# Expert rows that carry their destination: the per-tile results of a mixture of experts scattered by GpSimd instead of gathered per batch

## The chip, the cores and the metric

The kernel runs on one core of a Trainium2 chip. The metric is the device time of one launch in microseconds, the median of several runs. The engines of a core work side by side and meet at semaphores: TensorE (PE, with its weight loads PEld), VectorE (DVE), ScalarE (ACT), GpSimd (POOL) and SyncE (SP, which only starts transfers). 16 DMA engines move the data.

## The reference

The input is 16 batches of 256 tokens of 128 numbers. Four layers follow, each with a residual and a layer norm:

```
x = norm(x + attention0(x))     # MLP in front, 16 heads of 64, keys up to 63 ahead of the query
x = norm(x + experts(x))        # 16 experts, the best 4 of each token, 128 -> 512 -> 128, gelu
x = norm(x + attention1(x))     # 16 heads of 8, projections with a low-rank part, full softmax
x = norm(x + recurrent(x))      # gated state carried over the batches, tanh output
```

The expert layer computes, for each token, four expert results and their sum weighted by a softmax of the four router values.

## The kernel before

**Stage A, first attention and routing (about 30 to 671 us of the profile).** A loop over 16 batches `b`, each in eight steps `p` (a pair of heads each). In a step PE computes the scores of the pair (L804), the next q and k (L752, L753), in even steps the output projection of two older pairs (L821, which reads `OT`), the transposes of the normalized `P` of the step before (L841), and in odd steps P times V (L859). DVE copies `PTA` to `PT` (L1323), in even steps then `OTB` to `OT` (L1327), takes minima and shifted scores (L1335), and gives `rinv` (L1349, L1369). ACT takes the exponentials (L1165). POOL multiplies `P` by `rinv` (L555, three instructions in a step; PE's L841 of the next step waits for them). In steps 3 to 7 the finished batch is normalized and routed: DVE finds the four experts of a token (`hot`), its rank in each and from that its row in `xs` (`pos`), a table in DRAM with a region for each expert, and in step 7 writes `pos`, `pos_all` and the gates `gate_all` (L1411, L1413). In steps 0 to 3 of the following batch POOL issues eight indirect DMAs that scatter the 128-number rows of `x1c` to `xs` (L545, two in a step, ahead of the step's `P`).

**Stage B, experts (about 693 to 975 us).** DVE plans 144 tiles of 128 rows of one expert. SP loads a tile of rows (`load_rows`, L423), PE transposes it (L905) and multiplies it with the expert's two matrices (L917 and, two tiles later, L928). DVE copies the weights (`wA`, `wB`; L1487, L1490), the transposed rows (L1494), and adds the bias to the result `yrow` (L1516). SP stores `yrow` back over the same rows of `xs` (`store_rows`, L429). POOL clears buffers for stage C, one piece a tile, and gathers the results of batches 0 to 3 with indirect DMAs, paced by DVE's tile counter (L599). SP stores and loads the first stack of stage C at tiles 95 and 98 to 102.

**Stage C, second attention and recurrent layer (about 975 to 1417 us).** A loop over batches with eight steps of two heads. q and k of batch `b + 2` are split into three bf16 parts, stored to DRAM (`store_parts`, L439, four DMAs), and read back as a stack (`load_stack`, L446 to L456, nine DMAs into `qst`, `kst` or, for every third batch, into a part of `wall`). The scores of the next iteration start when the stack has landed (L1029); its step 1 computes the next q and k (L981), so stack, projection, parts, store and load are a loop. POOL's `outputs` fetches eight blocks of 128 expert results for one batch (`fetch`, L599, four at a time), ACT weighs them (L1241), POOL sums them (`combine`).

SP, POOL and the other engines take their instructions in order, so an instruction that waits holds all behind it. Two waits matter here:

```
DVE tile(n): need(dve, "hid_ready", 4 * n - 4); weights_A; rows_T; yrow of tile n - 2; weights_B
DVE tile(n): need(dve, "ys_out", tile n - 6)    # four yrow buffers
```

Of the kernel before, what the change touches and what calls it, by code (L numbers as in the profile page):

```python
# [36 lines left out]
LEVELS = TOK // GT  # L37
WA = F + FC
# [74 lines left out]
def build(nc, t, out):  # L113
    ctx = ExitStack()
    with ctx:
# [13 lines left out]
        pos_all = sb("pos_all", [128, B * TT * TOPK], u32)  # L129
# [10 lines left out]
        upto = sb("upto", [128, LEVELS])  # L140
        ended = sb("ended", [128, 2, LEVELS])
        spent = sb("spent", [128, 2, LEVELS])
# [9 lines left out]
        plan = sb("plan", [1, 512], i32)  # L152
        zrow = sb("zrow", [128, D])
        minus_half = sb("minus_half", [128, 8])

# [8 lines left out]
        hT = sb("hT", [128, TOK], c=a)  # L164
        h1 = sb("h1", [128, 2, 512], c=a)
# [13 lines left out]
        x1c = sb("x1c", [128, TT, D], c=a)  # L179
# [34 lines left out]
        lesser = sb("lesser", [128, LEVELS, E], c=a)  # L214
        a.close()
# [27 lines left out]
        posc = sb("posc", [128, 2, TT * TOPK // 2], u32)  # L243
# [16 lines left out]
        xg = sb("xg", [128, 4, D], c=e2)  # L260
# [3 lines left out]
        hid = sb("hid", [128, 4, FC, GT], c=e2)  # L264
        yrow = sb("yrow", [128, 4, D], c=e2)
# [25 lines left out]
        def rows_of(b):  # L291

            return h1[:, 0, :].rearrange("q (i d) -> q i d", d=D)[:, 0:TT, :] if isinstance(b, int) and b == B - 1 else x1c

        xs = nc.dram_tensor("xs", (ROWS, D), fp32, kind="Internal").ap()
# [7 lines left out]
            var_ready pow_ready x1c_ready m_x x1T_ready m_l mask_ready m_r pos_ready xsq_ready x1_kept scat exp_w top_ready  # L303
            ksq_ready rmat_ready b2_kept a_done plan_ready zrow_ready plan_out plan_in filled
# [3 lines left out]
            yk_in0 yk_in1 gates_in weighed comb_done var2_ready pow2_ready posc_ready xo_kept h_full fin_dve fin_pool var3_ready pow3_ready scale_ready h_act fin_ready out_done""".split()  # L308
# [65 lines left out]
        def _(sp):  # L374
# [17 lines left out]
            nothing = zrow[:, :].rearrange("q (o d) -> q o d", o=1).to_broadcast([128, E, D])  # L392
            for c in range(CAP // 128):
                if c % 2 == 0 and c > 0:
                    sp.wait_ge(s["filled"], 16 * c)
                if c >= 4:
                    sp.wait_ge(s["wo_mm"], PAIRS * (c // 2 - 1))
                sp.dma_start(rows[128 * c:128 * c + 128, :, :], nothing).then_inc(s["filled"], 16)
            sp.dma_start(xs[DUMMY:ROWS, :].rearrange("(e r) d -> r e d", r=128), nothing[:, 0:NT - FULL, :]).then_inc(s["filled"], 16)
# [9 lines left out]
            sp.dma_start(plan[:, :], plan_d.rearrange("(o t) c -> o (t c)", o=1)).then_inc(s["plan_in"], 16)  # L409
            sp.wait_ge(s["plan_in"], 16)  # L410
            sp.wait_ge(s["filled"], 16 * (CAP // 128 + 1))
# [6 lines left out]
            row = {}  # L418

            def load_rows(n):  # L420
                need_alone(sp, "tin_mm", n - 3)
                row[n] = row_of(n)
                sp.dma_start(xg[:, n % 4, :], xs[bass.ds(row[n], GT), :]).then_inc(s[f"xg_in{n % 4}"], 16)  # L423

            def store_rows(n):

                need_alone(sp, "yrow_ready", n + 1)
                need_alone(sp, f"ys_out{n % 2}", 16 * (n // 2))
                sp.dma_start(xs[bass.ds(row[n], GT), :], yrow[:, n % 4, :]).then_inc(s[f"ys_out{n % 2}"], 16)  # L429
# [11 lines left out]
            def load_stack(b, load, pair):  # L441

                if pair == 0:
# [3 lines left out]
                for w, x in ((1, kst), (0, qst)):  # L447
                    dst = x[load][2 * DH1 * pair:2 * DH1 * (pair + 1), :, :].rearrange("q (e h) n -> q e (h n)", e=2)
                    rows = qkd[w].rearrange("e a (d h) n -> (a d) e (h n)", h=H1 // 2)
                    first, second = PRODUCTS[pair][0][w], PRODUCTS[pair][1][w]  # L450
                    if first == second:
                        for e in range(2):
                            src = rows[DH1 * first:DH1 * (first + 1), e, :].rearrange("(o q) n -> o q n", o=1).to_broadcast([2, DH1, H1 // 2 * N])
                            sp.dma_start(dst[:, e, :], src).then_inc(s["stk"], 16)  # L454
                    else:
                        sp.dma_start(dst, rows[DH1 * first:DH1 * (second + 1), :, :]).then_inc(s["stk"], 16)  # L456

            for n in range(4):
                row[n] = row_of(n)
            sp.wait_ge(s["scat"], 16 * B * TT * TOPK)  # L460
            for n in range(4):
                sp.dma_start(xg[:, n, :], xs[bass.ds(row[n], GT), :]).then_inc(s[f"xg_in{n}"], 16)
            for n in range(NT + 4):
# [9 lines left out]
                if n in (98, 100, 102):  # L473
                    load_stack(-2, 0, (n - 98) // 2)

            def attention(b, par):
                if has(b, 2):
# [3 lines left out]
                    for qa in range(NPART):  # L481
                        load_stack(b, (par + 2) % 3, qa)
# [1242 lines left out]
```

## Time and profile before

| what | value |
|---|---|
| median of 3 runs | 1420.69 us (1418.19 to 1424.83) |
| the profiled execution | 1418.6 us, span 1416.9 us |
| busy in the span | PE 1261.3, PEld 969.5, DVE 1021.7, ACT 931.6, POOL 774.8 us |
| DMA | 110.98 MB, q1 (SP) 22.4% and q0 (POOL) 4.2% of 16 engines' span |
| chain that ended last | PE 25%, DMA 11%, SP's queue 6%, DVE 5% of the span |

The time that a row gives is from the span's start. A row of the timeline has start, length, engine, line, operation, tiles and count, and in brackets the idle time before it and what ended that. The chain of work that ended last is followed back from the last instruction; what stands in it at a time is what held the end there.

### The profile page before, as it was taken

To read this page: it belongs to the slowest core of one execution; us is meant where nothing else is said; L and a number is where in the kernel's file an instruction comes from. 1 tells how busy PE (TensorE), PEld (TensorE's weight loads), DVE (VectorE), ACT (ScalarE), POOL (GpSimd) and SP (SyncE) were. 2 spreads that over 40 slices of the span, in tenths; PEclk is the share of its full clock that TensorE was granted. 3 is DMA by queue.
4 is the path that set the end of the run, shared out by engine and by line. 5 is a ranking of instruction groups with operands and counts; after the bars stand their busy time and mean duration, and the time that the engine had idled before them with its cause. 6 is when DMAs were issued, how large, how long until landed. Compare 5 with 4: busy or idle time off the path is not lost.

```text
span 1416.9 us, 36694 instructions
## 1 busy us (share of the span) xinstructions
PE 1261.3 (89%) x9756; PEld 969.5 (68%) x9756; DVE 1021.7 (72%) x3767; ACT 931.6 (66%) x2827; POOL 774.8 (55%) x983
## 2 busy tenths in 40 slices
PE   7999999999999999996699999898687888888884
PEld 3777777677767777764599999897355555556552
DVE  1677777777777777775677777577678887878845
ACT  5877777777778777774366666464456665666554
POOL 1557777777777777775331131215547777674232
PEclk9999999999999999998799999999789999999997
DMA  9612222111222222221122222323223232322102
GB/s 338 219 61 76 74 74 74 59 43 54 70 73 71 74 74 74 74 71 50 45 72 74 82 81 79 93 75 82 67 70 82 64 85 52 91 58 74 40 2 60
DMA packets 149016, 110.98 MB, mean 78 GB/s; under 512 B 12833, under 2 KB 137249, under 8 KB 148770
## 3 DMA queue, kind: packets, MB, share of 16 engines
q1 hardware_dynamic: 139842, 92.45, 22.4%
q0 software_dynamic: 8192, 16.79, 4.2%
q8 instruction: 46, 0.75, 0.2%
q14 instruction: 72, 0.59, 0.1%
q10 hardware_dynamic: 864, 0.39, 0.1%
HBM read 47.27 MB, written 61.93 MB: 77 GB/s over the span
## 4 chain that ended last, share of the span: by engine, by line
PE 25%; DMA 11%; SPq 6%; DVE 5%; issue 2%; DVEq 1%; ACT 1%; ACTq 0%; POOL 0%; POOLq 0%
PE psum L917 9%; PE psum L928 9%; DMA qst<-qkd 4%; DMA wall<-qkd 3%; SPq L454 3%; DMA qkd<-parts 2%; SPq L439 2%; SPq L456 1%; PE psum L1029 1%; PE psum L905 1%; PE psum L941 1%; DVE mx L1526 1%; DVE parts L1593 1%; PE psum L981 1%; PE psum L953 1%
## 5 line engine op out<-in xcount | busy, mean ns | idle before, releaser
L555 POOL TENSOR_SCALAR P<-P,rinv 128x192 f32<-128x192 f32 (+1 forms) x384 | 309.2, 818 | 159.3 <-DVE rinv L1349 157.6
L1165 ACT ACTIVATE P<-shifted,least 128x192 f32<-128x192 f32 (+1 forms) x512 | 240.2, 470 | 113.8 <-DVE least L1335 112.5
L1187 ACT ACTIVATE hid<-psum,wA 128x128 f32<-128x128 f32 x576 | 165.0, 368 | 120.7 <-PE psum L917 120.7
L1526 DVE TENSOR_REDUCE mx<-psum 128x2 f32<-128x512 f32 x256 | 164.4, 685 | 41.1 <-PE psum L1029 33.1
L1335 DVE CUSTOM_DVE_ANT_0 shifted<-psum,band 128x192 f32<-128x192 f32 (+1 forms) x512 | 168.9, 384 | 31.4 <-PE psum L804 31.1
L599 POOL DMA_INDIRECT yk<-xs,posc x128 | 125.1, 977 | 104.6 <-DVE wA L1487 55.4
L1195 ACT ACTIVATE wall<-psum 128x1024 f32<-128x1024 f32 x128 | 130.7, 1021 | 77.4 <-PE psum L941 76.4
L917 PE MATMUL psum<-xgT,wA 128*128 128x128 f32 x1152 | 155.4, 279 | 0.6 <-DVE xgT L1494 0.6
L928 PE MATMUL psum<-wB,hid 128*128 128x128 f32 x1152 | 152.6, 276 | 0.0
L917 PEld LDWEIGHTS psum<-xgT,wA 128*128 128x128 f32 x1152 | 143.2, 195 | 1.3 <-issue 0.7
L545 POOL DMA_INDIRECT xs<-x1c,pos x120 | 120.5, 1004 | 39.0 <-issue 34.4
L841 PEld LDWEIGHTS psum<-ident,P 128*128 128x128 f32 x1024 | 117.1, 141 | 36.0 <-issue 29.1
L928 PEld LDWEIGHTS psum<-wB,hid 128*128 128x128 f32 x1152 | 140.6, 193 | 0.0
L841 PE MATMUL psum<-ident,P 128*128 128x128 f32 x1024 | 134.6, 274 | 3.7 <-POOL P L555 1.6
L804 PE MATMUL psum<-kT,qT 64*128 64x192 f32 (+1 forms) x1024 | 131.5, 375 | 0.6 <-DVE least L1335 0.6
L859 PE MATMUL psum<-PT,V 128*64 128x256 f32 (+1 forms) x1024 | 113.6, 365 | 0.7 <-DVE PT L1323 0.7
L804 PEld LDWEIGHTS psum<-kT,qT 64*128 64x128 f32 x1024 | 80.2, 186 | 38.6 <-issue 36.9
L1165 ACT ACTIVATION_READ_ACCUMULATOR P<-shifted,least 128x1 f32 x512 | 95.8, 187 | 0.0
L1487 DVE COPY wA<-wall 128x516 f32 x144 | 63.0, 437 | 41.5 <-ACT hid L1187 31.7
L859 PEld LDWEIGHTS psum<-PT,V 128*64 128x64 f32 x1024 | 69.2, 139 | 31.4 <-issue 9.5
L752 PE MATMUL psum<-hT,wg 128*128 (+1 forms) x256 | 88.9, 429 | 0.9 <-ACT kT L1122 0.9
L1490 DVE COPY wB<-wall 128x640 f32 x144 | 74.2, 515 | 20.9 <-DVE yrow L1516 1.5
(262 smaller groups left out, 2546.4 us busy)
## 6 DMA issues: line engine op xcount, KB each, us to landing
xs<-zrow SPq DMA_DIRECT2D x34, 1024.0 KB
xg<-xs SPq DMA_DIRECT2D x144, 64.0 KB, 1.8
xs<-yrow SPq DMA_DIRECT2D x144, 64.0 KB
wall<-in_wall SPq DMA_DIRECT2D x1, 8232.0 KB, 36.7
qkd<-parts SPq DMA_DIRECT2D x64, 96.0 KB
kst<-qkd SPq DMA_DIRECT2D x22, 128.0 KB
qst<-qkd SPq DMA_DIRECT2D x22, 128.0 KB
wall<-qkd SPq DMA_DIRECT2D x20, 128.0 KB
```

Of the source, the lines that this page charges most:

```text
L555: g.tensor_scalar(x, x, rinv[:, par, n:n + 1], None, ALU.mult).then_inc(s["pn_ready"], 1)
L599: g.indirect_dma_start(out=yk[:, slot, count * half + n, :], out_offset=None, in_=xs, in_offset=bass.IndirectOffsetOnAxis(posc[:, half, n: ...
L804: last = mm(bk[:, c0:c0 + w], qT[64 * h:64 * h + 64, p, it * 128:(it + 1) * 128], kT[64 * h:64 * h + 64, p, 0:w], start=True, stop=True)
L841: last = nc.tensor.transpose(bk[:, c0:c0 + 128], P[:, par1, it, h, jt * 128:(jt + 1) * 128], ident[:, :])
L859: last = mm(OTB[64 * h:64 * h + 64, k * N + c0:k * N + N], V[:, jt, r * 128 + 64 * h:r * 128 + 64 * h + 64], PT[:, k, h, keys], start=(jt ...
L917: mm(up(n, f), wA[:, n % 4, f * 128:(f + 1) * 128], xgT[:, n % 4, :], start=True, stop=True).then_inc(s["up_mm"], 1)
L928: last = mm(DN[n % 2][:, 0:D], hid[:, m, f, :], wB[:, m, f * D:(f + 1) * D], start=(f == 0), stop=(f == FC - 1))
L1165: last = sc.activation(P[:, par, it, h, 0:w], shifted[:, par, it, h, 0:w], ACT.Exp, scale=-1.0, bias=least[:, par, n:n + 1], accum_out=row ...
L1187: sc.activation(hid[:, n % 4, f, :], up(n, f), ACT.Gelu, bias=wA[:, n % 4, F + f:F + f + 1]).then_inc(s["hid_ready"], 1)
L1195: sc.activation(pc[:, p % 4, :, :, :].rearrange("q h j n -> q (h j n)"), ST, ACT.Exp, scale=SCALE1).then_inc(s["exps1"], 1)
L1335: v.tensor_tensor_reduce(out=shifted[:, par, it, h, 0:w], in0=bk[:, c0:c0 + w], in1=band[:, it, 0:w], scale=-SCALE0, scalar=3.0e38, op0=AL ...
L1526: v.tensor_reduce(out=mx[:, :, h], in_=SB[(par + 1 + h) % 3].rearrange("q (i n) -> q i n", i=TT), axis=mybir.AxisListType.X, op=ALU.max).t ...
```

## The change

- A row in `xs` grows from 128 to 144 numbers (`RC = D + E`). The last 16 hold, for each expert, the destination of the row: token times 4 plus the choice that took this expert. POOL works them out once a batch, in step 7, and they travel with the scatter of stage A. Empty rows hold destinations in a spill area (`SPILL`).
- In stage B DVE copies the column of the tile's expert into `slot_of` (`slot_in`), one instruction a tile. The results go no longer back to `xs` by SP, but by one indirect DMA of POOL a tile (`scatter`) to `yd`, a table in the order of tokens. POOL's clearing and summing pieces stand behind it, one a tile. SP keeps the loads of rows, with six instead of four row buffers.
- The eight gathers of a batch are gone. SP fetches a batch of `yd` with one plain DMA of 512 KB (`fetch`), in stage B at tiles 40, 72, 104 and 136, in stage C once the batch's stack has landed and ahead of `store_parts`. `load_stack` is cut into seven pieces, in stage B at every second tile from 98 to 110.
- In stage A, DVE copies `OT` ahead of `PT` in even steps, `pos_all` is gone, and the gates are computed in step 1 of the next batch.
- The plan's load is shorter; `row_of` is read beside each load instead of four ahead.

```diff
 # stage A, DVE
+                    if p % 2 == 0 and is_pair(b, p, -4):
+                        need(dve, "pv_mm", pair(b, p, -2))
+                        need(dve, "wo_mm", pair(b, p, -4))
+                        v.tensor_copy(OT[:, :, :].rearrange("q k n -> q (k n)"), OTB[:, :]).then_inc(s["ot_ev"], 2)
                     if is_pair(b, p, -2):
...
                         v.tensor_copy(PT[:, par, 0, WINDOW:2 * N], PTA[:, WINDOW:2 * N]).then_inc(s["ptA_ev"], 1)
-                    if p % 2 == 0 and is_pair(b, p, -4):
...
+                    if p == 1 and is_batch(b, -2):
+                        gates(b, 2)
...
                         v.tensor_copy(pos[:, :], posf[:, :]).then_inc(s["pos_ready"], 1)
-                        v.tensor_copy(pos_all[:, bass.ds((b - 1) * TT * TOPK, TT * TOPK)], posf[:, :])
-                        for it in range(TT):
-                            v.tensor_scalar(gate_all[...], wexp[:, it, :], wsum[:, it:it + 1], None, ALU.mult)
 # stage A, POOL
+                            need_alone(pool, "slot_ready", b - 1)
...
+                    if p == 7 and is_batch(b, -1):
+                        need_alone(pool, "mask_ready", b)
+                        for it in range(TT):
+                            g.tensor_scalar(chosen_slot[:, it, :], hot[:, it, 3, :], 3.0, slots[:, it:it + 1], ALU.mult, ALU.add)
+                        g.drain()
+                        g.tensor_tensor(chosen_slot[:, :, :], chosen_slot[:, :, :], hot[:, :, 1, :], ALU.add)
+                        g.drain()
+                        g.tensor_tensor(chosen_slot[:, :, :], chosen_slot[:, :, :], hot[:, :, 2, :], ALU.add)
+                        g.drain()
+                        g.tensor_tensor(rows_of(b - 1)[:, :, D:RC], chosen_slot[:, :, :], hot[:, :, 2, :], ALU.add).then_inc(s["slot_ready"], 1)
+                        g.tensor_scalar(slots[:, :], slots[:, :], float(N * TOPK), None, ALU.add)
 # stage B, DVE
+            def slot_in(n, e):
+                v.tensor_copy(slot_of[:, n % SL:n % SL + 1], xg[:, n % XG, bass.ds(e + D, 1)]).then_inc(s["slot_in"], 1)
...
                     rows_T(n + 2, q)
+                    slot_in(n + 2, e)
 # stage B, POOL (fetch, fetch_paced, at_tile and next_tile are gone)
+            def scatter(n):
+                need_alone(pool, "yrow_ready", n + 1)
+                need_alone(pool, f"ys_out{n % 2}", 16 * (n // 2))
+                g.indirect_dma_start(out=yd, out_offset=bass.IndirectOffsetOnAxis(slot_of[:, n % SL:n % SL + 1].bitcast(u32), 0),
+                                     in_=yrow[:, n % 4, :], in_offset=None).then_inc(s[f"ys_out{n % 2}"], 16)
+            for n in range(NT):
+                scatter(n)
+                clear_ahead(n)
...
 # SP
+            def fetch(b, par):
+                need_alone(sp, "comb_done", b + 2)
+                sp.dma_start(yk[:, (par + 1) % 3, :, :], yd[bass.ds(SPILL + (b + 4) * N * TOPK, N * TOPK), :].rearrange("(q n) d -> q n d", n=TT * TOPK)).then_inc(s["yk_in"], 16)
+            def stored(n):
+                for k in range(2):
+                    sp.wait_ge(s[f"ys_out{k}"], 8 * n)
...
-                if n >= 4:
-                    store_rows(n - 4)
...
-                if n in (98, 100, 102):
+                if 98 <= n < 98 + 14 and n % 2 == 0:
                     load_stack(-2, 0, (n - 98) // 2)
+                for b, at in ((-4, 40), (-3, 72), (-2, 104), (-1, 136)):
+                    if n == at:
+                        stored(at - 8)
+                        fetch(b, b % 3)
+            stored(NT)
             def attention(b, par):
+                if has(b, 4) and not (isinstance(b, int) and b < 0):
+                    need_alone(sp, "stk", 16 * NSTK * (b + 2))
+                    fetch(b, par)
                 if has(b, 2):
```

## Rows read from the trace of the kernel before

**Rows 1.** Busy by stretch: length, PE, PEld, DVE, ACT, POOL, clock, DMA, GB/s.
```profile
30.00:671.00 641.00, 611.89 (x4369) 442.72 (x4367) 467.18 (x2089) 477.47 (x1662) 451.85 (x550) 0.99 0.25 79
693.00:974.00 281.00, 275.39 (x2421) 274.31 (x2422) 204.17 (x592) 171.44 (x598) 64.19 (x89) 0.98 0.28 79
```

**Rows 2.** What PE waited for in stage A (us in total, times, longest).
```profile
PE psum L821 <- DVE OT L1327: 12.1, 17, 1.0
```

**Rows 3.** Timeline of stage A around the start of one batch.
```profile
418.98 2.43 POOL L555 TENSOR_SCALAR P<-P,rinv 128x192 f32<-128x192 f32 x3 [2.56 <-DVE rinv L1349]
...
422.07 1.09 POOL L545 DMA_INDIRECT xs<-x1c,pos  x1 [0.66 <-issue]
422.42 0.68 DVE L1327 COPY OT<-psum 128x512 f32<-128x512 f32 x1
...
423.15 1.16 PE L821 MATMUL psum<-wo,OT 128*128 128x128 f32 x8 [0.77 <-DVE OT L1327]
...
424.85 2.41 POOL L555 TENSOR_SCALAR P<-P,rinv 128x192 f32<-128x192 f32 x3 [0.42 <-DVE rinv L1349]
...
434.70 2.41 POOL L555 TENSOR_SCALAR P<-P,rinv 128x192 f32<-128x192 f32 x3
...
437.10 1.04 PE L841 MATMUL psum<-ident,P 128*128 128x128 f32 x8
```

**Rows 4.** Timeline: POOL's small instruction, an indirect DMA behind its semaphore.
```profile
1105.33 0.19 POOL L596 COPY posc<-pos_all 128x4 uint32 x1
1106.34 1.05 POOL L599 DMA_INDIRECT yk<-xs,posc  x1 [0.83 <-POOL posc L596]
```

**Rows 5.** Groups by shape: POOL's tensor_tensor behind a drain (busy, mean, idle).
```profile
L644 POOL TENSOR_TENSOR c<-c,tf 128x256 f32<-128x256 f32 x14 | 10.2, 731 | 2.1 <-issue 0.2
```

**Rows 6.** Timeline of DVE in stage B: small instructions; wA to wA.
```profile
834.33 0.17 DVE L93 TENSOR_SCALAR nh<-mv 128x2 f32<-128x2 f32 x1
834.41 0.16 DVE L94 TENSOR_SCALAR ve<-mv 128x2 f32<-128x2 f32 x1
...
940.55 0.43 DVE L1487 COPY wA<-wall 128x516 f32 x1 [0.27 <-ACT hid L1187]
...
942.28 0.43 DVE L1487 COPY wA<-wall 128x516 f32 x1 [0.27 <-ACT hid L1187]
```

**Rows 7.** Timeline of PE in stage B: one tile's transpose and the next one's.
```profile
882.03 0.27 PE L905 MATMUL psum<-ident,xg 128*128 128x128 f32 x1
...
883.93 0.27 PE L905 MATMUL psum<-ident,xg 128*128 128x128 f32 x1
```

**Rows 8.** Who waited for whom, 693 to 974 us (us in total, times, longest).
```profile
PE psum L905 <- DMA xg<-xs: 5.4, 3, 2.4
```

**Rows 9.** POOL's gathers: duration in ns, min/median/max.
```profile
L599 POOL DMA_INDIRECT yk<-xs,posc x128: 941/955/1196, 773.3 to 1279.8; - x128
```

**Rows 10.** Timeline: POOL's last scatter of stage A.
```profile
686.82 0.96 POOL L545 DMA_INDIRECT xs<-h,pos  x1 [0.30 <-issue]
```

**Rows 11.** DMA queues, 688.3 to 688.8 us (packets, MB, share of 16 engines).
```profile
q0 software_dynamic: 32, 0.07, 40.9%
```

**Rows 12.** DMA queues, 1110.12 to 1122.54 us, a stack load of stage C.
```profile
q0 software_dynamic: 192, 0.39, 12.3%
```

**Rows 13.** Chain that ended last: the stack's last DMA in two iterations.
```profile
1115.24 7.29 DMA qst<-qkd
...
1307.91 6.29 DMA wall<-qkd
```

**Rows 14.** Busy by stretch (as Rows 1): twelve iterations, one without gathers.
```profile
982.95:1276.11 293.16, 230.82 (x1955) 154.75 (x1956) 230.81 (x659) 177.31 (x361) 191.07 (x253) 0.93 0.30 72
...
1276.11:1298.13 22.02, 19.29 (x176) 13.59 (x175) 19.11 (x58) 15.40 (x33) 12.66 (x16) 1.00 0.28 69
```

**Rows 15.** What PE waited for in stage C (us in total, times, longest).
```profile
PE psum L1029 <- DMA qst<-qkd: 20.7, 9, 6.3
```

**Rows 16.** DMA issues: a plain 512 KB load (KB, us to landing).
```profile
hT<-in_xT SPq DMA_DIRECT2D x4, 512.0 KB, 5.4
```

More of the change, by code:

```diff
@@ L37 @@
 LEVELS = TOK // GT
+RC = D + E
+SPILL = 2 * E * GT
+XG = 6
+SL = 16
 WA = F + FC
@@ L446, in load_stack @@
                     sp.dma_start(qst[load][MROW:MROW + NPART, :, :].rearrange("q (e h) n -> q e (h n)", e=2), no_maxima).then_inc(s["stk"], 16)
[L447 to L459, printed above, removed]
+                    return
+                pair, w = (piece - 1) // 2, piece % 2
+                dst = (qst, kst)[w][load][2 * DH1 * pair:2 * DH1 * (pair + 1), :, :].rearrange("q (e h) n -> q e (h n)", e=2)
+                rows = qkd[w].rearrange("e a (d h) n -> (a d) e (h n)", h=H1 // 2)
+                first, second = PRODUCTS[pair][0][w], PRODUCTS[pair][1][w]
+                if first == second:
+                    for e in range(2):
+                        src = rows[DH1 * first:DH1 * (first + 1), e, :].rearrange("(o q) n -> o q n", o=1).to_broadcast([2, DH1, H1 // 2 * N])
+                        sp.dma_start(dst[:, e, :], src).then_inc(s["stk"], 16)
+                else:
+                    sp.dma_start(dst, rows[DH1 * first:DH1 * (second + 1), :, :]).then_inc(s["stk"], 16)
             sp.wait_ge(s["scat"], 16 * B * TT * TOPK)
             for n in range(4):
-                sp.dma_start(xg[:, n, :], xs[bass.ds(row[n], GT), :]).then_inc(s[f"xg_in{n}"], 16)
-            for n in range(NT + 4):
+                load_rows(n)
+            for n in range(NT):
                 if n + 4 < NT:
                     load_rows(n + 4)
-                if n >= 4:
-                    store_rows(n - 4)
                 if n == 95:
@@ L1237, in weigh @@
                 slot, count = (par + 1) % 3, TT * TOPK // 2
-                need(act, f"yk_in{half}", 16 * count * (b + 5))
+                need(act, "yk_in", 16 * (b + 5))
                 need(act, "gates_in", b + 5)
@@ L1310, in _, with gates @@
                 v.tensor_tensor(V[:, jt, 0:512], M[:, :], bv[:, 0:512], ALU.add).then_inc(s["v_ev"], 1)
+            def gates(b, back):
+                need(dve, "exp_w", b - back + 1)
+                v.reciprocal(wsum[:, :], wsum[:, :])
+                v.drain()
+                for it in range(TT):
+                    last = v.tensor_scalar(gate_all[:, bass.ds(b - back, 1), it * TOPK:(it + 1) * TOPK].rearrange("q o k -> q (o k)"), wexp[:, it, :], wsum[:, it:it + 1], None, ALU.mult)
+                last.then_inc(s["gate_ready"], 1)
             def values(n, half, jt):
@@ L1410, in body @@
                         v.tensor_copy(pos[:, :], posf[:, :]).then_inc(s["pos_ready"], 1)
[L1411 to L1413 removed]
+                        if isinstance(b, int) and b == B:
+                            gates(b, 1)
             batch_loop(dve, 2, B - 1, 2, body)
```

225 lines of the change are left out of this document (96 added, 129 removed).

## The prediction

> **What bounds the kernel now.** I read the busy time by stretch first, then who waited for whom in each stretch, then the timelines where the change cuts in, and last the chain that ended last. In stage B PE is busy 275.4 of 281.0 us [rows 1], so there a tile costs what PE needs: 1.90 us from one transpose to the next [rows 7], 144 tiles 273 us. In stage A too PE is the bound: 611.9 of 641.0 us, with POOL at 452 us on average [rows 1]. But POOL's work is uneven: in steps 0 to 3 two indirect DMAs stand in front of each pair's `P`, and there it runs without a gap. In stage C the chain goes through SP's queue and the stack's transfers: an iteration ends when the stack has landed, 7.29 us behind its last DMA [rows 13], and PE stands before L1029 for it, 20.7 us in 9 times for two of the three buffers alone [rows 15]. In stage C any time taken off the transfers shortens the loop; in A and B only what lets PE go on does.
>
> **Stage A, DVE's order.** At the start of a batch PE stands 0.77 us at L821 until `OT` is copied at 423.10 [rows 3]; in total 12.1 us in 17 waits [rows 2]. With `OT` first, and the gates (moved to step 1, where POOL's queue is far enough behind to hide them) and `pos_all` out of step 7, the copy ends before PE asks. That alone would give 0.77 us a batch. `PT` comes up to 0.7 us later in even steps, ahead of transposes that start over 2 us later; I count nothing for it.
>
> **Stage A, POOL's slots.** The new block stands between `P` of step 7, which ends at 421.41 (418.98 + 2.43), and the first scatter, which started at 422.07, 0.66 us behind [rows 3]. It is two tensor_scalars of 16 columns, three tensor_tensors of 32 and three drains, and then the scatter waits for the last one's semaphore. The trace has no such instruction of POOL. A copy of 4 columns is 0.19 us [rows 4], a tensor_tensor of 256 columns 0.73 us [rows 5]; 32 columns lie near the first, so I take 0.2 each, 1.0 for five. A drain leaves 0.15 us (2.1 us in 14) [rows 5], three 0.45. From the small instruction's end to the indirect DMA behind its semaphore are 0.83 us [rows 4]. Sum 2.28 in place of 0.66, so the scatter starts 1.6 us later. POOL's idle 0.42 us before `P` of step 0 [rows 3] swallows a part, and 1.2 us stay, without another gap until `P` of step 3. `P` of step 2 ended at 437.11 (434.70 + 2.41); PE began its eight transposes at 437.10, and the second four, which need the third `P`, near 437.6 [rows 3]. In the new kernel that `P` ends at 438.3, so PE stands 0.7 us behind its old time, and the 0.77 us won at L821 are swallowed by this wait. In steps 4 to 7 POOL catches up, but PE does not. The loop has 14 batches with both scatter and pairs: **+10 us**.
> Bounds: with the block free and its latency hidden, POOL keeps its old times, and of the 0.77 us PE still loses 0.28 waiting for the same `P` (437.11 against 436.83): 14 times -0.49 is -7 us. With instructions and drains at twice my value the scatter is 3.07 late, `P` 2.65, PE 2.15: +30 us. At 0.73 us an instruction it would be +47; 16 and 32 columns are too far from 256 for that, and it stays outside the range.
>
> **Stage A, the rest.** Rows of 576 instead of 512 bytes, and the extra fill of 16 columns, lie on DMA engines that are busy a quarter of the time [rows 1]; nothing. The scatter instructions stay eight a batch. If the fill fell behind, POOL's wait for `filled` would hold the scatter; two chunks a batch are issued well ahead.
>
> **Stage B.** Removed are 144 plain stores from SP's queue, 32 gathers from POOL's. Late loads of rows, behind the stack's DMAs on that queue, cost PE 5.4 us in 3 waits [rows 8]. Without the stores SP is less full and the stack comes in seven pieces over fourteen tiles, so I take all of it off, -5. The fetches of 512 KB stand in front of row loads instead: 5.4 us to landing [rows 16] against four tiles of lead (7.6 us), so a load behind one is just in time; nothing, or 2 us each of four (+8) if it isn't.
> DVE gets `slot_in` behind `rows_T`. When it catches up it goes from wA to wA in 1.73 us (942.28 - 940.55) [rows 6], against PE's 1.90: 0.17 us to spare. Two small instructions start 0.08 us apart and take 0.17 [rows 6]. I take 0.1, which leaves 0.07 us a tile to recover from the norms that lie between tiles; they make it late for about a us, +1. Bounds: 0.08, nothing; 0.25 (a duration and a start), 1.98 us a tile, +12 us.
> POOL scatters once a tile: 0.96 us [rows 9] with up to 0.83 in front and a memset of 0.5 to 0.9 behind it in the first 31 tiles, about the tile's 1.9 us. It falls behind by a few us at most and four `yrow` buffers take that up: DVE asks for the scatter of tile n - 6. Nothing, or +3. Sum of B: **-4 us**, from -5 to +15.
> Behind the last tile POOL clears the third stack buffer some 10 us later than before; the stack of batch 0 isn't ready then anyway. SP's `stored(NT)` waits for the last scatter, less than 3 us behind its `yrow`, while the parts are still being made.
>
> **Stage C.** Here is what the change is worth. POOL's gathers run with the stack's load: in one load window the software queue moved 0.39 MB and took 12.3% of the engines [rows 12], and the last DMA landed after 7.29 us; in an iteration behind the last gather it was 6.29 [rows 13]. The twelve iterations with gathers took 293.16 us, 24.43 each; the first without, which still weighs, sums and normalizes as before, 22.02, with PE at 19.3 and DVE at 19.1 us [rows 14]. The plain fetch is issued when the stack has landed, takes some 5.4 us [rows 16], and the parts come later than that, so it meets neither store nor load. Twelve times 2.4 is 29 us. I take 2.0 each, because the twelve ran at a mean granted clock of 0.93 [rows 14], so part of the difference may be TensorE's slower start rather than gathers: **-24 us**. Bounds: 0, if the loop doesn't follow, and -29.
> Weighing waits for the fetch late in the iteration, over 5 us after it has landed. POOL is free of 8 us an iteration, which nothing waits for.
>
> **Sum.** 1418.6 us (span 1416.9 and 1.7 around it) + 10 - 4 - 24 = 1400.6. The median of the runs is 2.1 us above the profiled one: **1402 us**. A measurement of this kernel tells a change of about 0.5%, 7 us, from none.
>
> **The rivals.**
> *The slot block is hidden* (0.20). POOL's sequencer runs ahead of its engine, so drains and setup may overlap `P` of step 7. For it speaks that in steps 1 to 3 a scatter starts quickly behind `P`; against it that the block's instructions depend on each other. Then stage A gives -7 instead of +10: 1385 us.
> *Stage C doesn't shorten* (0.13). The loop of 22.02 us was seen once, behind the gathers, and the fetch now lies in the stretch where the row maxima's transfer goes out; if that comes late, PE stands in step 4, and DVE, at 19.1 of 22.0 us [rows 14], has little to give. Then -4 instead of -24: 1422 us, no change.
> *The scatter sets the tile's time* (0.12, slower). Scatter n waits until scatter n - 2 has landed. The last scatter of stage A ended at 687.78 [rows 10], and its packets ran before 688.8 [rows 11], so landing is 1.0 us: a pair needs 0.83 + 0.96 + 1.0, 1.4 us a tile, below 1.90. Under load it may be longer. From 2.0 us on it is the bound, and from 2.4 us on (2.1 a tile, +29) the kernel is slower than before; at 2.8 us it is 2.3 a tile, +58, 1460 us.
> A rule of the Trainium skill speaks for such a loss: by SBUF — State Buffer, section "SBUF: two separate sides", a VectorE copy in a two-port mode locks GpSimd out of the shared port, so that GpSimd can't write descriptors until it ends; wA and wB are such copies. By its example, a DMA of 0.62 us that takes 3.1, POOL would need 3.9 us a tile (estimate), some 290 us more. The trace disagrees: gathers issued beside these copies took at most 1.196 us, median 0.955 [rows 9], so I give the rule 0.02 of the 0.12.
> *The forecast* (0.55): 1392 to 1412 us.
>
> **Range and chances.** 1382 to 1420 us leaves out the scatter's case, a stage C without any gain, and the far end of the slot block. Faster by over 0.5% 0.75 (forecast and hidden block), same 0.13, slower 0.12.
>
> **What would show it.** In the new trace: L821 no longer waits for `OT`; PE waits at L841 for POOL's `P` once or twice a batch, 0.7 us or more; no wait of L905 for `xg`; wA to wA at 1.90 us or less; POOL's scatters at 0.96 us, one a tile; in stage C iterations of 22.0 to 22.5 us, with the fetch landed before the parts go out. The prediction is wrong if PE waits in stage B for DVE or DVE for `ys_out`, if the slot block takes under 1 or over 3 us, or if iterations stay at 24 us.

## The result, and the profile after

The changed kernel took 1456.5 us (median of 4, 1455.1 to 1457.9) against 1419.4 for the kernel before beside it: 1.026 times as long, 95% interval 1.024 to 1.027. The prediction was 1402 us, 17 less than before; it came out 37 more. The profiled execution took 1455.1 us with a span of 1453.3. Two executions of kernels of experiment 6, one of them profiled, took 3.4 and 3.9 ms; the times below leave them out, and nothing here explains them.

The times at which SP starts certain transfers cut the span into three stages. "A" ends with the plan's store, "B" runs from the first load of `xg` to the store of batch -1's parts, "C" from there to the end (us, one profiled execution each):

| kernel | plan stored | first `xg` | B | C |
|---|---|---|---|---|
| before | 683.4 | 690.1 | 292.8 | 434.0 |
| changed | 726.6 | 733.5 | 308.9 | 410.9 |
| difference | +43.2 | (+0.3 between) | +16.1 | -23.1 |

The prediction had +10, -4 and -24. The last is right; the loss is in A and B. Profiles of kernels whose code for a stage is the same tell how far such a difference can be read: stage A of the changed kernel and of five edits that leave it alone ends at 722.9 to 726.8 us, and a stage B that an edit leaves alone took 306.8 to 308.9 us in six profiles.

Busy by stretch in the changed kernel, columns as in [rows 1]: stage A, one batch of it, stage B, and the twelve iterations of stage C that answer to [rows 14].

```profile
30.00:714.00 684.00, 630.83 (x4367) 453.08 (x4365) 466.07 (x2074) 477.12 (x1662) 475.36 (x641) 0.96 0.27 82
...
401.07:443.39 42.32, 39.84 (x279) 28.83 (x277) 29.26 (x132) 30.10 (x107) 30.36 (x42) 0.96 0.24 70
...
735.00:1037.00 302.00, 287.76 (x2466) 281.55 (x2466) 223.72 (x742) 173.20 (x604) 178.95 (x192) 0.98 0.28 79
...
1042.43:1312.07 269.64, 220.44 (x1953) 150.96 (x1952) 223.48 (x657) 175.73 (x361) 101.72 (x139) 0.96 0.31 79
```

PE does 4367 matmuls between 30 and 714 us, where before it did 4369 between 30 and 671 [rows 1], 43 us less, so the same matmuls take 43 us longer; the granted clock fell from 0.99 to 0.96. In stage C the twelve iterations take 22.47 us each, against 24.43.

**Stage A.** The timeline around the start of a batch, as [rows 3]:

```profile
401.07 2.50 POOL L581 TENSOR_SCALAR P<-P,rinv 128x192 f32<-128x192 f32 x3 [2.56 <-DVE rinv L1361]
403.56 0.53 POOL L585 TENSOR_SCALAR chosen_slot<-hot,slots 128x16 f32<-128x16 f32 x2
404.92 0.25 POOL L587 TENSOR_TENSOR chosen_slot<-chosen_slot,hot 128x32 f32<-128x32 f32 x1 [0.83 <-issue]
405.31 0.25 POOL L589 TENSOR_TENSOR chosen_slot<-chosen_slot,hot 128x32 f32<-128x32 f32 x1
405.70 0.25 POOL L591 TENSOR_TENSOR x1c<-chosen_slot,hot 128x32 f32<-128x32 f32 x1
406.04 0.23 POOL L592 TENSOR_SCALAR slots<-slots 128x2 f32<-128x2 f32 x1
407.20 1.11 POOL L571 DMA_INDIRECT xs<-x1c,pos  x1 [0.93 <-issue]
...
409.62 2.44 POOL L581 TENSOR_SCALAR P<-P,rinv 128x192 f32<-128x192 f32 x3
...
411.38 1.97 PE L841 MATMUL psum<-ident,P 128*128 128x128 f32 x8 [2.16 <-POOL P L581]
413.29 2.36 PE L859 MATMUL psum<-PT,V 128*64 128x256 f32 x16
```

`P` of step 7 ends at 403.57, the scatter starts at 407.20: 3.63 us behind, where before it was 0.66 [rows 3]. The `P` of step 0 begins at 409.62 without a gap, and PE stands 2.16 us for it. Its next 24 matmuls then run slowly: eight transposes in 1.97 us where 1.04 is usual [rows 3], the sixteen of L859 in 2.36. The windows view shows the clock beside it: PE is busy throughout until 409, stands, and then gets a clock of 0.50, which is 1.2 of 2.4 GHz, and 0.71 in the stretch after; from 415.6 on it is 1.00 again.

```profile
401.00:409.00 8.00, 8.00 (x58) 5.60 (x54) 6.17 (x26) 5.91 (x21) 5.50 (x11) 1.00 0.03 8
409.20:411.30 2.10, 0.02 (x1) 0.00 (x0) 1.46 (x9) 2.10 (x9) 2.05 (x3) 0.97 0.10 35
411.40:413.30 1.90, 1.90 (x10) 1.55 (x10) 0.00 (x0) 0.03 (x1) 1.70 (x2) 0.50 0.00 0
413.30:415.50 2.20, 2.20 (x17) 1.36 (x16) 0.00 (x0) 0.51 (x2) 1.89 (x3) 0.71 0.21 67
```

What PE waited for from 30 to 714 us; `OT`'s 12.1 us in 17 waits [rows 2] are nearly gone, the wait for POOL is new:

```profile
PE psum L841 <- POOL P L581: 31.4, 15, 3.0
...
PE psum L821 <- DVE OT L1333: 2.6, 2, 1.8
```

**Stage B.** The timeline of two tiles where POOL still clears the stack buffers. `wA` takes 0.95 us in place of 0.43 [rows 6], the memset beside it 1.19, and the tiles are 2.31 us apart (792.51 less 790.20), not 1.90 [rows 7]:

```profile
790.20 1.16 PE L917 MATMUL psum<-xgT,wA 128*128 128x128 f32 x8 [0.15 <-DVE xgT L1504]
...
790.54 0.55 DVE L1500 COPY wB<-wall 128x640 f32 x1
790.79 1.19 POOL L606 MEMSET kst<- 3x1024 bf16 x1
...
791.30 0.95 DVE L1497 COPY wA<-wall 128x516 f32 x1 [0.22 <-issue]
792.14 0.96 POOL L700 DMA_INDIRECT yd<-yrow,slot_of  x1 [0.17 <-issue]
...
792.51 1.16 PE L917 MATMUL psum<-xgT,wA 128*128 128x128 f32 x8
```

The timeline at a combine. POOL stands 3.02 and 2.62 us in front of two additions with no releaser shown ("issue"); each of them has a drain ahead of it, and ahead of the drain a scatter. VectorE waits 4.22 us for the second sum:

```profile
874.02 1.05 POOL L700 DMA_INDIRECT yd<-yrow,slot_of  x1 [0.17 <-issue]
878.09 1.00 POOL L675 TENSOR_TENSOR sums<-yk 128x256 f32<-128x256 f32 x1 [3.02 <-issue]
879.25 1.21 POOL L700 DMA_INDIRECT yd<-yrow,slot_of  x1 [0.16 <-issue]
883.08 0.71 POOL L677 TENSOR_TENSOR sums<-sums,x_all 128x256 f32<-128x256 f32 x1 [2.62 <-issue]
...
883.83 0.49 DVE L88 BATCH_NORM_STATS2 st<-sums 128x6 f32<-128x128 f32 x2 [4.22 <-POOL sums L677]
```

Who waited for whom from 735 to 1037 us, and POOL's scatters of stage B (min, median, max in ns), which answer to the gathers of [rows 9]:

```profile
DVE yrow L1532 <- DMA yd<-yrow,slot_of: 12.1, 10, 3.1
...
POOL sums L675 <- issue: 10.1, 3, 4.3
POOL sums L677 <- issue: 7.9, 3, 3.7
PE psum L917 <- DVE xgT L1504: 9.2, 15, 3.5
```

```profile
L700 POOL DMA_INDIRECT yd<-yrow,slot_of x143: 952/964/1346, 744.8 to 1038.3; - x143
```

The scatters themselves cost what was assumed, 0.96 us. What is late is what stands behind drains. Two of the signs by which the prediction called itself wrong are in these rows: PE waits in stage B for DVE (9.2 us in 15 waits), and DVE for `ys_out` (12.1 us in 10).

### The profile page after: what moved, and what is told of

It is laid out like the page before. It is cut to its first block, busy times and chain, and to the rows that moved or that the text cites. A ratio compares the mean times of both kernels' runs of the same rounds, so it can differ in the third digit from the quotient of the medians.

```text
span 1453.3 us, 36975 instructions
## 1 busy us (share of the span) xinstructions
PE 1278.8 (88%) x9756; PEld 979.5 (67%) x9756; DVE 1032.5 (71%) x3895; ACT 929.2 (64%) x2827; POOL 816.9 (56%) x1067
## 4 chain that ended last, share of the span: by engine, by line
DMA 13%; PE 13%; issue 7%; SPq 5%; DVE 5%; POOL 3%; DVEq 2%; ACT 1%; POOLq 1%; ACTq 0%
DMA yd<-yrow,slot_of 4%; DMA qst<-qkd 4%; PE psum L917 4%; PE psum L928 3%; DMA wall<-qkd 2%; SPq L468 2%; DMA qkd<-parts 2%; SPq L452 2%; POOL yd L700 2%; DVE mx L1542 1%; SPq L470 1%; PE psum L1029 1%; PE psum L941 1%; DVE parts L1609 1%; PE psum L981 1%
## 5 line engine op out<-in xcount | busy, mean ns | idle before, releaser
L700 POOL DMA_INDIRECT yd<-yrow,slot_of x144 | 143.4, 996 | 104.1 <-DVE yrow L1532 55.5
L841 PE MATMUL psum<-ident,P 128*128 128x128 f32 x1024 | 142.6, 283 | 34.4 <-POOL P L581 31.4
L841 PEld LDWEIGHTS psum<-ident,P 128*128 128x128 f32 x1024 | 120.3, 145 | 73.0 <-POOL P L581 41.2
L804 PE MATMUL psum<-kT,qT 64*128 64x192 f32 (+1 forms) x1024 | 134.7, 383 | 0.6 <-DVE least L1345 0.6
L859 PE MATMUL psum<-PT,V 128*64 128x256 f32 (+1 forms) x1024 | 122.1, 385 | 0.7 <-DVE PT L1337 0.7
L619 POOL TENSOR_TENSOR rstd<-ve,minus_half 128x4 f32<-128x4 f32 (+1 forms) x20 | 18.7, 933 | 163.2 <-DVE ve L98 163.1
L1333 DVE COPY OT<-psum 128x512 f32<-128x512 f32 x64 | 44.1, 690 | 86.9 <-PE psum L859 81.2
L1151 ACT ACTIVATE PT<-psum 128x448 f32<-128x448 f32 x128 | 68.5, 535 | 55.8 <-PE psum L859 44.4
L1497 DVE COPY wA<-wall 128x516 f32 x144 | 72.1, 501 | 37.5 <-issue 23.4
L859 PEld LDWEIGHTS psum<-PT,V 128*64 128x64 f32 x1024 | 73.3, 147 | 35.5 <-issue 14.0
```

The lines of the kernel that those rows point to most:

```text
L700: g.indirect_dma_start(out=yd, out_offset=bass.IndirectOffsetOnAxis(slot_of[:, n % SL:n % SL + 1].bitcast(u32), 0), in_=yrow[:, n % 4, :], ...
L804: last = mm(bk[:, c0:c0 + w], qT[64 * h:64 * h + 64, p, it * 128:(it + 1) * 128], kT[64 * h:64 * h + 64, p, 0:w], start=True, stop=True)
L841: last = nc.tensor.transpose(bk[:, c0:c0 + 128], P[:, par1, it, h, jt * 128:(jt + 1) * 128], ident[:, :])
L859: last = mm(OTB[64 * h:64 * h + 64, k * N + c0:k * N + N], V[:, jt, r * 128 + 64 * h:r * 128 + 64 * h + 64], PT[:, k, h, keys], start=(jt ...
```

## The experiments

"Before" is beside each as measured on the same chip; every kernel but one (experiment 2) is an edit of the changed one. "Kernel 1" is the kernel of experiment 1, and so on. The stages come from one profiled execution each.

**1. The slot block in front of `P` of step 7.** There POOL waits 2.56 us for `rinv` in every batch.

```diff
                     if is_pair(b, p, 0):          # POOL: P of this step
-                    if p == 7 and is_batch(b, -1):
-                        need_alone(pool, "mask_ready", b)
-                        ...                        # the slot block, behind P
+                    (the same block stands ahead of "if is_pair(b, p, 0)")
```

> The changed kernel with POOL's slot block moved from behind the P of step 7 to in front of it, where POOL idles 2.56 us for rinv in the changed kernel's trace. Theory: the block stands between P and the first scatter (3.63 us instead of 0.66), makes the P of step 0 late, and PE's wait for it (2.2 us) and the low granted clock behind it are the whole loss of stage A. Then the batch falls from 42.6 us to 39.3 or less, stage A loses its 43 us, and the kernel takes 1408 to 1418 us. Rival: the loss comes from VectorE's new order or from the wider rows; then most of it stays and the kernel takes over 1435 us.

Measured: 1402.3 us (before 1421.7; ratio 0.987, 0.984 to 0.989), faster by more than the theory allowed. The plan is stored at 673.9: stage A is 52.7 us shorter than in the changed kernel and 9.5 shorter than before; B (308.8) and C (410.0) stay. POOL's timeline at the end of a batch:

```profile
408.74 2.40 POOL L592 TENSOR_SCALAR P<-P,rinv 128x192 f32<-128x192 f32 x3 [2.50 <-DVE rinv L1361]
411.13 0.54 POOL L577 TENSOR_SCALAR chosen_slot<-hot,slots 128x16 f32<-128x16 f32 x2
412.49 0.25 POOL L579 TENSOR_TENSOR chosen_slot<-chosen_slot,hot 128x32 f32<-128x32 f32 x1 [0.82 <-issue]
...
413.94 2.48 POOL L592 TENSOR_SCALAR P<-P,rinv 128x192 f32<-128x192 f32 x3
...
416.83 1.10 POOL L571 DMA_INDIRECT xs<-x1c,pos  x1 [0.41 <-issue]
```

The same instructions, as long as before, fill the gap, and the scatter follows `P` after 0.41 us. The slot block's place was the whole loss of stage A; with the wider rows and VectorE's order still in it, stage A is shorter than before.

**2. VectorE's order alone**, in the kernel before.

```diff
+                    if p % 2 == 0 and is_pair(b, p, -4):   # OT, as it stood below
+                        ...
                     if is_pair(b, p, -2):                  # PT
                         ...
-                    if p % 2 == 0 and is_pair(b, p, -4):
-                        ...
```

> The kernel before with one edit of the change, OT copied ahead of PT by VectorE. The prediction's step: 0.77 us a batch at L821, of which 0.28 comes back as a wait for POOL's P unless more gives way: 7 to 11 us less, 1409 to 1412 us. Rival: PT now comes later and PE waits for it or for POOL's P instead; no gain, 1419 us, or a loss.

Measured: 1415.7 us (before 1421.7; ratio 0.996, 0.994 to 0.998), 6 us less and so a little short of the 7 to 11 expected. Stage A is 4.1 us shorter in the profiled executions, and a batch, from its first scatter to the next one's, takes 39.05 us for 39.37 before. `OT` is still late, 5.2 us in 14 waits, since `pos_all` and the gates stay in step 7:

```profile
PE psum L821 <- DVE OT L1323: 5.2, 14, 0.9
```

A batch of kernel 1 takes 38.63 us, so the swap is 0.32 of the 0.74 us gained there; that the rest comes from what left step 7 is argued from this row, not tried alone.

**3. No drain between the scatters.**

```diff
-                    g.tensor_tensor(y4[..0:2..], y4[..0:2..], y4[..2:4..], ALU.add)
+                    g.tensor_tensor(y4[..0:2..], y4[..0:2..], y4[..2:4..], ALU.add).then_inc(s["ahead"], 1)
                 else:
-                    g.drain()
+                    pool.wait_ge(s["ahead"], 3 * (b + 4) + piece)
```

and the three drains of `clear_ahead` in the same way.

> The changed kernel with the nine drains that POOL has between its scatters in stage B replaced by waits on a semaphore of the operation that they are for. Theory: a drain behind a running indirect DMA lasts until that DMA has landed (2.6 to 3.7 us in the trace), which makes the combined rows late for VectorE and PE; about 8 to 10 us of stage B's 16 go, 1447 us. Rival: the scatters themselves, or their landing, are what is late; then nothing changes, 1456 us.

Measured: 1442.6 us (before 1421.7; ratio 1.015, 1.013 to 1.018), 14 less than the changed kernel. Stage B is 293.9 us, 1.1 more than before: all of its loss but 1 us is gone, more than the 8 to 10 us expected. The combine's additions now follow the scatters at once:

```profile
870.50 0.99 POOL L700 DMA_INDIRECT yd<-yrow,slot_of  x1 [0.16 <-issue]
871.51 0.99 POOL L675 TENSOR_TENSOR sums<-yk 128x256 f32<-128x256 f32 x1
872.66 0.99 POOL L700 DMA_INDIRECT yd<-yrow,slot_of  x1 [0.16 <-issue]
873.68 0.98 POOL L677 TENSOR_TENSOR sums<-sums,x_all 128x256 f32<-128x256 f32 x1
```

and of VectorE's 12.1 us behind the scatters little is left (waits from 735 to 1027 us in this kernel):

```profile
DVE yrow L1532 <- DMA yd<-yrow,slot_of: 0.8, 1, 0.8
```

**4. Only the combine's six drains replaced.**

> The changed kernel with only the six drains of combine_ahead replaced by semaphores; the three of clear_ahead stay. The extra time between wA copies of the changed kernel lies at the combine's tiles (about 4.6 us near tile 70, 3 near tile 135) and at tiles 31 to 42, behind the clearing's drains (about 4). Theory: 8 to 10 of the 14 us go, 1447 us, the rest belongs to the clearing. Rival: the combine is all of it, 1443 us.

Measured: 1448.2 us (before 1420.1; ratio 1.020, 1.018 to 1.022), 8 less than the changed kernel. Stage B is 299.2 us: by the profiles 9.7 of its 16 us were the combine's drains, 5.3 more the clearing's three, each good to the 2 us by which equal stages B differ. The whole time doesn't check this split: the profiled execution has a stage A 3.7 us shorter, without any edit there, and a stage C of 417.5 for 410.9 us. There POOL stands 9.35 us in front of its first memset (L601) with no releaser shown, where it is 1.91 us in the changed kernel, and nothing here explains it.

**5. Memsets in halves, each behind a `wA`.**

```diff
+                pool.wait_ge(s["wA_ready"], piece + 6)
-                    g.memset(x[:, h:h + 4, :] ..., 0.0)
+                    g.memset(x[:, h:h + 2, :] ..., 0.0)
```

The edit also takes the pieces in another order and has two drains in the clearing where the changed kernel has three.

> The changed kernel with the memsets of stage B cut in halves and each started behind the wA copy of VectorE instead of right behind a scatter. Theory: memset and wA copy run at the same time and stretch each other (wA 0.95 instead of 0.43 us, memset 1.19 instead of 0.94), a tile then takes 2.31 us instead of 1.90 in about 10 tiles; 4 us go, 1452 us, and no wA copy over 0.6 us is left in the stretch of the memsets. Rival: the stretch comes from the scatter's descriptors; then wA stays at 0.95 in places and the tiles at 2.3.

Measured: 1453.6 us (before 1421.7; ratio 1.022, 1.020 to 1.024); stage B 307.1 us. From 735 to 840 us `wA` takes 0.456 us on average where kernel 3, with the memsets as the change has them, has 0.555:

```profile
L1498 DVE COPY wA<-wall 128x516 f32 x51 | 23.2, 456 | 12.4 <-ACT hid L1189 11.3 <-issue 0.9
```

The mechanism is mostly as expected: the copies are short again, but for one of 0.79 us. The effect is small. The median is 2.9 us below the changed kernel's, the intervals of the two ratios overlap slightly, and stage B lies within the spread of stages B that nothing changed; one drain fewer would also give something. So what the pacing is worth isn't shown beyond "at most 3 us", and kernel 3 shows that stage B can afford the stretched copies.

**6. Delays in place of the block.** Kernel 1 with 2, 4 or 7 memsets into an unused tile in front of the batch's first scatter.

```diff
                         if p == 0:
+                            for k in range(2):     # 4, 7
+                                g.memset(pad[:, k, :], 0.0)
                             need_alone(pool, "pos_ready", b - 1)
```

> The changed kernel with the slot block moved (1402.3 us), and two memsets of about 0.53 us each put in front of the first scatter of every batch: the scatters, and the P of steps 0 to 3, come about 1.0 us later. By the prediction's step (0.42 us of POOL's idle time and some of PE's slack swallow the first part, then one for one): 0 to 0.6 us a batch, 1402 to 1411 us. Rival: PE has no slack left and loses one for one and more: 1.0 us or more a batch, 1417 us or above.

> As before with four such memsets, about 2.1 us. By the prediction's step one for one behind the slack: 1.1 to 1.7 us a batch, 1418 to 1426 us. Rival: a wait of PE at the P of step 0 costs more than its length, since the granted clock is low behind it (0.77 to 0.80 in the changed kernel's trace): 2.5 us or more a batch, 1437 us or above. The changed kernel itself, 3.2 us later than the moved block, lost 3.9 a batch.

> The changed kernel with the slot block moved (1402.3 us) and seven memsets of about 0.5 us in front of the first scatter of every batch: some 3.2 us later, as late as the slot block makes it in the changed kernel. The first two delays cost 1.09 and 1.10 us a batch for each us of delay (0.68 us: 10.3 us; 1.67 us: 25.8 us). If lateness is all that the slot block does, this kernel takes as long as the changed one, 1452 to 1459 us; at the slope of the short delays it would be 1450 us, and what lies above is the low granted clock behind PE's longer wait. Rival: the block also does something else to the batch (VectorE's hot held until slot_ready, a port shared with VectorE); then the pure delay stays below 1448 us.

| kernel | scatter behind `P` of step 7 | time | batch at full clock | batches with a low clock |
|---|---|---|---|---|
| before | 0.66 us | 1419.4 us | 39.37 us | |
| kernel 1 | 0.41 | 1402.3 | 38.63 | |
| 2 memsets | 1.11 | 1412.6 | 39.36 | |
| 4 memsets | about 2.1, by their number | 1428.1 | not profiled | |
| 7 memsets | 3.44 | 1458.8 | 41.67 | 42.96 |
| changed kernel | 3.63 | 1456.5 | 41.73 (kernel 4) | 42.33 or 42.98 |

A batch runs from its first scatter to the next one's; between 150 and 580 us the batches of one kind agree within 0.1 us. Here are one batch at full clock of kernel 1, of the kernels with 2 and with 7 memsets, and of kernel 4, whose stage A is that of the changed kernel:

```profile
416.83:455.46 38.63, 38.23 (x277) 27.87 (x276) 29.16 (x132) 30.11 (x105) 30.30 (x42) 1.00 0.26 76
```

```profile
422.83:462.19 39.36, 38.76 (x278) 27.76 (x277) 29.45 (x132) 30.23 (x105) 31.27 (x44) 1.00 0.25 75
```

```profile
405.47:447.14 41.67, 38.84 (x277) 27.75 (x279) 29.79 (x132) 30.21 (x107) 33.58 (x48) 1.00 0.23 71
```

```profile
406.02:447.75 41.73, 38.97 (x277) 27.71 (x277) 29.88 (x133) 30.25 (x106) 30.35 (x41) 1.00 0.23 71
```

Against kernel 1 a delay of 0.70 us costs 0.73 us a batch, 3.03 us cost 3.04, and the block's 3.22 cost 3.1: one for one, from the first on. The expected slack of 0.42 us was refuted by the first kernel. The pure delay costs as much as the block, so lateness is all that the block does. (The medians give more, 1.1 to 1.3 us for each us over 14 batches; the first and last batches have the memsets too, and some batches the low clock.)

The low clock comes on top. Between 150 and 580 us a batch with a stretch of it takes 0.6 or 1.3 us more than one without, in all seven profiles with a late scatter. In the changed kernel's profile twelve of the thirteen batches from 109 to 663 us have one, about 11 us in all; in kernel 4's, with the same stage A, six have one, about 7 us, and its plan is stored 3.7 us earlier. PE waits with seven memsets as in the changed kernel:

```profile
PE psum L844 <- POOL P L595: 32.5, 14, 3.3
```

**7. The plain fetch with the stack's load.**

```diff
-                    need_alone(sp, "stk", 16 * NSTK * (b + 2))
-                    fetch(b, par)                  # behind the landed stack
                     store_parts(b)
+                    fetch(b, par)                  # ahead of load_stack
```

> The changed kernel with the plain fetch of 512 KB in the loop of stage C issued behind the parts' store and so together with the stack's load, in place of behind the landed stack. What made the stack's load long before was the gathers beside it. Theory 1, bytes: 0.5 MB beside the load makes it as long again, iterations of about 24 us, 1474 us. Theory 2, it was the gathers as such (their many descriptors, or POOL's time): the plain fetch costs less than 0.7 us an iteration, 1457 to 1465 us.

Measured: 1461.7 us (before 1418.8; ratio 1.030, 1.028 to 1.032), 5 more than the changed kernel. The profiled execution was the longest, 1467.8; in it the twelve iterations take 23.87 us each:

```profile
1039.58:1325.98 286.40, 232.19 (x1953) 156.44 (x1952) 224.30 (x657) 176.64 (x361) 101.66 (x139) 0.91 0.30 73
```

By the medians it is 0.4 us an iteration, as theory 2 had it; by the profile 1.4. The stack lands after 6.7 to 8.6 us in this profile, 6.8 to 7.4 in the changed kernel's. Bytes beside the load cost something, and this run doesn't say how much of a gather's price they are.

**8. Gathers put back.** Eight a batch of 128 rows, where the kernel before had them, into a tile nobody reads; the computation is not touched. The rows gathered are fixed ones of 576 bytes from the start of `xs`, and the plain fetch stays, so more bytes move than before (28.1 MB in the twelve iterations, 21.1 before).

```diff
+                    for n in range(count * half, count * (half + 1)):
+                        g.indirect_dma_start(out=spoil[:, n % count, :], out_offset=None, in_=xs,
+                                             in_offset=bass.IndirectOffsetOnAxis(pick[:, n:n + 1], 0)).then_inc(s["jg_in"], 16)
```

> The changed kernel with eight gathers of 128 rows put back on POOL in each of the twelve iterations, where the kernel before had them, into a tile that nobody reads; the plain fetch stays. Theory: gathers beside the stack's load are what made an iteration of stage C 24.4 us instead of 22.5; they do so again: 24 us or more, 1475 to 1482 us. Rival: the iteration was longer for the wait on the gathered rows (which nothing waits for here), or for POOL's time in front of its combine; then 22.5 stays, 1457 to 1462 us.

Measured: 1479.2 us (before 1420.1; ratio 1.042, 1.038 to 1.045), 23 more than the changed kernel. The windows view of the twelve iterations, 24.85 us each:

```profile
1038.80:1337.01 298.21, 230.49 (x1952) 155.53 (x1951) 227.86 (x657) 177.12 (x361) 195.07 (x233) 0.92 0.39 94
```

and from the chain that ended last, parts landing and then the stack, first in the changed kernel, then in this one:

```profile
1111.66 2.23 DMA qkd<-parts
1118.32 7.36 DMA qst<-qkd
```

```profile
1121.07 8.57 DMA qst<-qkd
...
1138.88 4.20 DMA qkd<-parts
```

No engine waits for these gathers' data, and the iteration is as long as before the change. The edit puts POOL's time back too, so the run alone doesn't refute that rival; its trace does: nothing of POOL stands in the chain that ended last in these iterations, and PE and VectorE wait for nothing of POOL. So it is the gathers beside the transfers (the stack's landing, 6.8 to 7.4 us in the changed kernel, is 7.5 to 8.7), as the prediction had it. How much of it is their bytes, and how much TensorE's granted clock (0.92 here, 0.96 in the changed kernel), stays open.

**9. Slot block moved, no drains**; with the memsets as they are ("both") and in halves ("both_paced"). The second also writes the rows of ones as f32 instead of bf16 (0.58 us a memset for 1.15) and has one wait more, for `gates_in`.

> The changed kernel with the slot block in front of the P of step 7 and no drain between the scatters, memsets as the change has them. If the memsets matter as much as alone (3 us, 1.8 of them in stage B), 1389 us against 1386.7 with paced memsets; if the drains were all of it, 1387 us.

> The changed kernel with the slot block in front of the P of step 7, no drain between the scatters, and the memsets of stage B in halves behind the wA copies. If the three causes are apart, their gains add: 1456.5 - 54 - 14 - 3 = 1385 us (1382 to 1389), 34 us below the kernel before. If stage B is bound by something common (the scatters on POOL), the last two overlap and it stays at 1388 or above.

Measured: 1388.9 us (before 1420.1; ratio 0.979, 0.977 to 0.982) and 1386.7 us (before 1418.8; ratio 0.977, 0.976 to 0.978). The gains of moving the block and of replacing the drains add: 1456.5 less 54.2 and 13.8 is 1388.5. The second kernel is the fastest, 2.3% below the one before and 4.8% below the changed one; its stages are plan at 674.4, B 291.3, C 411.3. That it is faster than the first isn't shown (the intervals overlap), and what it gains isn't the pacing alone.

## Why the prediction was wrong

The prediction's own sum is 1402.7 us, written as 1402; nothing hangs on it.

**Stage C (-24, measured -23.1): right**, with the gathers beside the transfers as the cause (their bytes or the clock: open, experiment 8), and the iterations of 22.0 to 22.5 us that it named. Where the plain fetch lies is worth another 0.4 us an iteration or more.

**Stage A, VectorE's order: right.** With the block hidden the prediction had -7 us, 0.49 a batch; kernel 1's stage A gave -9.5, 0.74 a batch.

**Stage A, the slot block (+10, measured +43): the failed step.** Three things in it:
- *The price.* The prediction had 2.28 us from the end of `P` to the scatter; it is 3.63. The small instructions take 0.25 us, not 0.2, and there are six: `slots` is advanced too, 0.23 us, which the sum left out though the diff has it. The first of the three drains leaves 0.83 us (the other two 0.14, as assumed), and the wait ahead of the scatter 0.93 for 0.83. That is 3.0 us late in place of 1.6, what the prediction called "twice my value" and priced at +30, an end that the range left out.
- *POOL's slack.* 0.42 us of POOL's idle time were taken off, then 0.5 of PE's. The second holds as far as these runs tell (it is the 0.49 us a batch of the prediction's lower bound). The first doesn't: a batch with two memsets, whose scatter comes 0.45 us later than in the kernel before, takes 39.36 us against 39.37, so the 0.74 us gained in kernel 1 are gone, while by the prediction's rule almost 0.5 should be left. In kernel 1 the gap is no longer there: the second scatter ends at 419.20 and `P` of step 0 starts at 419.24. That `rinv` comes earlier because PE does, now that `OT` is on time, is argued, not tried.
- *The clock.* The sum for stage A had no term for it. PE's wait of 2.16 us is followed by matmuls that take some 1.5 us longer (0.93 at L841, 0.6 at L859 against the 1.73 us of kernel 1). Part of that fills a wait that would have come anyway, for the `P` of steps 1 to 3 are as late: a batch with a low clock is 0.6 or 1.3 us longer than one without (experiment 6), about 11 us in all in the changed kernel's profile.

In numbers: at full clock a batch is 41.7 us, 2.3 more than before, where the prediction had 0.7. Of the difference 1.35 are the price and 0.3 POOL's slack. Over 14 batches that is 10 as predicted, 19 for the price, 4 for the slack, and 11 for the clock: 44, measured 43.2.

The prediction also placed PE's wait at the `P` of step 2; it came at step 0, the first one behind the block.

**Stage B (-4, measured +16): a cost that was not in the sum.** The prediction counted scatter, memset and copy, and looked for a bound per tile. The nine drains that the change spreads between scatters have no term in it; the only price of a drain in the prediction, 0.15 us [rows 5], is that of one behind an addition. Behind an indirect DMA a drain holds POOL until that DMA has landed or longer: POOL idles 1.6 to 4.3 us before these nine, three of them end 0.1 us behind the landing and six 0.3 to 1.6 us behind it. The trace of the kernel before had this price too. In its stage C the drain ahead of L633 stands behind four gathers, and POOL idles 24.4 us in front of 13 of these additions (groups by shape):

```profile
L633 POOL TENSOR_TENSOR sums<-yk 128x256 f32<-128x256 f32 x13 | 9.5, 729 | 24.4 <-issue 24.4
```

The same drain without gathers ahead of it leaves 0.15 us in the changed kernel. PE and VectorE waited for nothing of POOL there, so it cost nothing; in stage B VectorE waits. The nine drains made the combine's sums late for VectorE, and through `ys_out` its `yrow`. Of 16.1 us the combine's drains are 9.7, the clearing's 5.3, each give or take 2; 1.1 are left for `slot_in` and the rest. Kernel 3 has a scatter in every tile and a stage B as long as before, so the rival "the scatter sets the tile's time" is refuted, though its sign was the right one.

The lock rule of the Trainium skill (SBUF — State Buffer, "SBUF: two separate sides": of a VectorE copy in a two-port mode and a GpSimd instruction, the one that starts first keeps the shared port until it ends) was given 0.02. For descriptors the trace still disagrees: the scatters beside VectorE's copies take 0.964 us in the median, 1.346 at most. For memset and copy the trace agrees with it. The memset starts 0.30 us before `wB` ends and ends 0.89 us after that; `wA`, issued in that time, ends 0.27 us behind the memset: each seems to stand until the other is through. Pacing the memsets takes most of it away and is worth 3 us at most (experiments 5 and 9).

## What to carry to other kernels

A drain left 0.14 to 0.83 us behind short work, but held POOL for at least the whole landing behind an indirect DMA: between DMAs, order an engine's own operations by a semaphore of the operation that is meant. Before adding work to a queue, look for the place where that queue already waits for something later, here 2.56 us ahead of `P` in the same step, and put it there; the same six instructions cost 53 us of stage A in one place and nothing in the other. And an idle stretch in the old trace needn't be slack in the new kernel: when one engine is made earlier, ask of every gap what ended it, and whether that comes earlier too.

## What was not expected of the hardware

A chain of 32-column additions on POOL starts one every 0.39 us with a drain in between, but the first drain behind two tensor_scalars leaves 0.82 us. A wait of PE of 2.16 us behind a stretch at full clock was followed by 1.9 us at half of it; with seven memsets a wait of 2.25 us at the same place was followed by matmuls at full speed (1.39 us at L844, 1.73 at L862). In the changed kernel's profile nearly every batch got the low clock, in other profiles of the same stage A from half of them to nearly all, and nothing here tells which will. A plain transfer of 512 KB beside the stack's load cost 0.4 to 1.4 us an iteration, eight gathers of about as many bytes 2.4.
